# Four fused transformer layers on one core: shared experts with inner units in partitions, placed earlier, and the last gathers beside the attention

## The reference, cut to what matters

```python
sh = silu(x @ sh_gate) * (x @ sh_up) @ sh_down * sigmoid(x @ sh_gate_w)        # layer 2
z  = silu(xf @ Ws1 + bs1) * (xf @ Ws11 + bs11) @ Ws2 + bs2                      # layer 3
h  = silu(xf @ W1[e] + b1[e]) * (xf @ W11[e] + b11[e])                          # expert e
y  = y + (h @ W2[e] + b2[e]) * gates[:, e, None]
```

## Time and profile before

| what | us |
|---|---|
| median of 3 runs | 1956.16 (1954.9 to 1962.01) |
| the profiled execution | 1963.65 |
| its span, first to last instruction | 1961.8 |
| PE busy | 1400.3 (71%) |
| DVE busy | 1314.5 (67%) |
| ACT busy | 957.5 (49%) |
| POOL busy | 297.2 (15%) |

### The profile page before, as it was taken

How to read it: one execution, slowest core, us unless ns; L and a number is a source line. 1 busy time by engine, 2 the same in 40 slices (tenths; PEclk the granted TensorE clock), 3 DMA queues, 4 the chain that set the end, 5 groups by cost and what they waited for, 6 DMA issues and landing times.

```text
span 1961.8 us, 22511 instructions
## 1 busy us (share of the span) xinstructions
PE 1400.3 (71%) x6402; PEld 623.9 (32%) x6402; DVE 1314.5 (67%) x4037; ACT 957.5 (49%) x2225; POOL 297.2 (15%) x388
## 2 busy tenths in 40 slices
PE   6788888873344410453488899878898699999984
PEld 2345444441111100210134555322232234434431
DVE  5989979887888876393265566677676454555552
ACT  3888878863444433121155455444443344444452
POOL 0201010010000000047410010245205201000014
PEclk7989989897555555555598899888786799899995
DMA  3010101004100000214122223223112601111111
GB/s 111 26 49 15 51 7 63 1 1 149 60 1 1 0 1 1 63 43 135 47 50 72 67 88 95 64 59 72 41 33 80 161 20 28 25 54 45 45 30 54
DMA packets 151441, 98.44 MB, mean 50 GB/s; under 512 B 73328, under 2 KB 136117, under 8 KB 151265
## 3 DMA queue, kind: packets, MB, share of 16 engines
q1 hardware_dynamic: 143543, 84.01, 14.7%
q0 software_dynamic: 6144, 12.60, 2.3%
q10 hardware_dynamic: 1632, 0.39, 0.1%
HBM read 60.83 MB, written 35.73 MB: 49 GB/s over the span
## 4 chain that ended last, share of the span: by engine, by line
PE 46%; DVE 33%; issue 9%; ACT 6%; another core or an unknown queue 4%; DMA 1%; SPq 1%; POOL 1%; DVEq 0%; ACTq 0%; POOLq 0%
PE PS L483 38%; DVE RA L1593 5%; DVE nmx L1346 4%; PE PS L479 4%; DVE RA L1595 4%; DVE RA L1150 3%; DVE RA L1153 3%; PE PS L831 2%; DVE RB L1153 1%; DVE RB L1150 1%; DVE RA L1309 1%; DVE RA L1311 1%; PE PS L820 1%; ACT RA L1737 1%
## 5 line engine op out<-in xcount | busy, mean ns | idle before, releaser
L483 PE MATMUL PS<-RA 72*128 72x512 bf16 (+2 forms) x1360 | 463.8, 429 | 148.6 <-DVE nmx L1346 92.7
L1346 DVE TENSOR_REDUCE nmx<-PS 128x1 f32<-128x512 f32 x512 | 348.2, 685 | 257.2 <-PE PS L483 167.0
L1791 ACT ACTIVATE RA<-PS 128x512 f32<-128x512 f32 x512 | 301.7, 598 | 337.5 <-PE PS L483 276.3
L483 PEld LDWEIGHTS PS<-RA 72*128 72x128 bf16 (+3 forms) x1360 | 120.3, 103 | 456.0 <-issue 204.3
L483 PE MATMUL PS<-RA,Vs 128*32 128x512 f32 x1240 | 225.1, 721 | 0.7 <-issue 0.7
L1919 ACT ACTIVATE RA<-RA 128x8 f32<-128x8 f32 x511 | 107.5, 210 | 168.1 <-DVE RA L1593 167.2
L479 PE MATMUL PS<-ident,RB 128*128 128x128 f32 (+1 forms) x329 | 63.1, 338 | 137.6 <-DVE RB L1525 123.3
L1971 POOL DMA_INDIRECT RA<-yd,RA x96 | 93.4, 973 | 431.8 <-DMA yd<-RA 271.1
L483 PE MATMUL PS<-RB,RA 128*128 (+2 forms) x672 | 152.5, 344 | 4.6 <-DVE RA L1326 4.6
L483 PE MATMUL PS<-RB 128*128 (+3 forms) x280 | 108.7, 524 | 43.0 <-ACT RB L1893 28.8
L1150 DVE TENSOR_SCALAR RA<-PS 128x1024 f32<-128x1024 f32 x96 | 117.0, 1219 | 24.3 <-PE PS L483 24.2
(11 more groups left out here) (299 smaller groups left out, 2037.5 us busy)
## 6 DMA issues: line engine op xcount, KB each, us to landing
RA<-scr SPq DMA_DIRECT2D x288, 96.0 KB
xd<-Otok SPq DMA_DIRECT2D x36, 256.0 KB, 3.2
RA<-xd SPq DMA_DIRECT2D x72, 128.0 KB, 2.3
scr<-parts SPq DMA_DIRECT2D x48, 128.0 KB
yd<-RB SPq DMA_DIRECT2D x48, 128.0 KB, 1.8
RB<-in_L_ffn_W SPq DMA_DIRECT2D x24, 256.0 KB
scr<-parts SPq DMA_DIRECT2D x64, 48.0 KB
yd<-RA SPq DMA_DIRECT2D x48, 64.0 KB, 1.5
```

Source lines behind the costliest of these rows:

```text
L483: return e.matmul(o, l, r, start=first, stop=last)
L1346: e.tensor_reduce(nmx[:, (g + lx) % 3, c:c + 1], bank[(6, 0)[i % 2]], AX.X, ALU.max, negate=True).then_inc(*ROWMAX.up(layer, n, i))
L1791: e.activation(chunk(layer, k, i), bank[(1, 5)[i % 2]], ACT.Exp).then_inc(*EXP.up(layer, k, i))
```

## The change

It does four things.

- **Form.** A shared item's `hidden` is now four matmuls, each with 128 columns of the weights as stationary operand and the 128 tokens moving, so that the inner units come out in partitions. In layer 3 each has a bias matmul of its own behind it. The result needs no transpose: `hturned` and its copy are gone for shared items, and `down` reads what DVE gated. Such an item has three steps now.
- **Place.** `spread` takes a part of the work, a first quarter, a rate, and the earliest quarter of a task. Layer 2's items end at quarter 174, and its gathers run at 0.95 a quarter from 180 to 252. Layer 3's first `hidden` stands at quarter 226, its next items at every third quarter from 256 to 322, and the last eight from 335 to 360. The routed items of layer 3 run at 1.75 steps a quarter from 361 to 473, its gathers from 479 to 518.
- **Norms.** `READY3` is computed as 208, 220, 236, 295: blocks 1 and 2 come 11 and 19 quarters earlier. All four blocks' features use bank 2.
- **Loads.** The three loads for the shared expert of layer 3 move to quarter 200 (`shared3`). The other 24 pieces are issued two a quarter, from 348 on.

```diff
     HT = RA[:, 9984:10496].rearrange("p (u c k) -> p u c k", u=2, c=2)
+    HTs = RA[:, 9984:10496].rearrange("p (u k) -> p u k", u=2)
...
-    READY3 = (208, 231, 255, 295)
-    FEATURES3 = (2, 2, 3, 4)
-    SPLIT3 = READY3[0] + 16
+    FEATURES3 = (2, 2, 2, 2)
...
-    def expert_steps(lx):
+    def expert_steps(lx, part):
 
         nsh, G, ni = len(shared[lx]), groups[lx], items[lx]
-        steps = [[("hidden", 0)], [("gated", 0)]]
-        for i in range(ni):
+        first, end = ((0, ni), ((0, nsh), (nsh, ni))[part])[lx]
+        steps = [[("rows", r)] for r in (0, 2) if first]
+        steps += [[("turned", first + u)] for u in range(2) if first]
+        steps += [[("hidden", first)], [("gated", first)]]
+        for i in range(first, end):
             r = G * (i - nsh + 4)
-            steps.append(([("rows", r)] if r >= 0 and r % 2 == 0 and r < ntiles[lx] else []) + [("hturned", i)])
-            steps.append([("hidden", i + 1)] if i + 1 < ni else [])
-            steps.append(([("gated", i + 1)] if i + 1 < ni else []) + ([("turned", i + 2)] if nsh <= i + 2 < ni else []))
+            fetch = [("rows", r)] if end > nsh and r >= 0 and r % 2 == 0 and r < ntiles[lx] else []
+            if i >= nsh:
+                steps.append([("hturned", i)])
+            steps.append(fetch + ([("hidden", i + 1)] if i + 1 < end else []))
+            steps.append(([("gated", i + 1)] if i + 1 < end else []) + ([("turned", i + 2)] if nsh <= i + 2 < end else []))
             steps.append([("down", i)])
...
-    plan = {2: spread(expert_steps(0), 14, 2.05), 3: spread(expert_steps(1), 27, 2.25)}
-    assert not plan[2][1]
-
+    def spread(layer, steps, at, rate, earliest=lambda task: 0):
+
+        credit = 0.0
+        for tasks in steps:
+            while credit < 1.0 or at <= max([earliest(t) for t in tasks], default=0):
+                credit = min(credit + rate, 1.0 + rate)
+                at += 1
+            credit -= 1.0
+            plan[layer].setdefault(divmod(at - 1, 4), []).extend(tasks)
+        return at
+
+    plan = {2: {}, 3: {}}
+    last = spread(2, expert_steps(0, 0), 56, 2.05)
+    assert spread(2, gather_steps(0), last + 4, 0.95) <= 4 * STEPS
+    added = [max(4 * n + i for (n, i), tasks in plan[2].items() for t in tasks if t[0] == "combine" and t[1] // 16 == b) for b in range(4)]
+    READY3 = [max(added[b], 4 * (16 * b + 25) + 2, 4 * (48 + LAG) - 9) + 1 for b in range(4)]
...
+        b = task[1] // 8
+        return READY3[b] + (10 if b < 3 else 40) - 4 * LEAD
+
+    spread(3, expert_steps(1, 0), READY3[0] + 18 - 4 * LEAD, 1.0, earliest)
+    last = spread(3, expert_steps(1, 1), READY3[3] + 65 - 4 * LEAD, 1.75)
+    assert spread(3, gather_steps(1), last + 4, 0.95) <= 4 * STEPS
...
                     n, wgu, f, down, be = shared[lx][i]
-                    ins = mm(bank[bk][:, 0:2 * f], XT[:, 128 * n:128 * n + 128], wgu, True, lx == 0)
                     if lx:
-                        ins = mm(bank[bk][:, 0:2 * f], SELB[:, 128 * be:128 * be + 128], BI[:, :], False, True)
+                        wait_xt(3, n // 4)
+                    for c in range(4):
+                        o = bank[bk][:, 128 * c:128 * c + 128]
+                        ins = mm(o, wgu[:, 128 * c:128 * c + 128], XT[:, 128 * n:128 * n + 128], True, lx == 0)
+                        if lx:
+                            ins = mm(o, BI[:, 128 * c:128 * c + 128], SELB[:, 128 * be:128 * be + 128], False, True)
...
-                pe.wait_ge(HT_A, lx, i)
+                pe.wait_ge(GATED if i < nsh else HT_A, lx, i)
...
-            weights(lx, 4 * n + i - ROUTE_LATE[layer] - LOAD_FROM)
-            for task in plan[layer][0].get((n, i), ()):
-                expert_step(lx, task)
+                if layer == 2 and n == 50:
+                    shared3()
+            at_ = 4 * n + i - ROUTE_LATE[layer] - LOAD_FROM
+            for piece in range(at_, at_ + 1) if lx == 0 else range(2 * at_, 2 * at_ + 2):
+                weights(lx, piece)
...
-            if i < 2:
-                e.dma_start(w3gu[:, 16:18, 256 * i:256 * i + 256], T["L3_ffn_" + ("Ws1", "Ws11")[i]].rearrange("h (s i) -> h s i", s=2)).then_inc(*W3S.up())
...
+        def shared3():
+
+            sp.wait_ge(DOWN, 0, items[0] - 1)
+            for i in range(2):
+                e.dma_start(w3gu[:, 16:18, 256 * i:256 * i + 256], T["L3_ffn_" + ("Ws1", "Ws11")[i]].rearrange("h (s i) -> h s i", s=2)).then_inc(*W3S.up())
+            e.dma_start(w3d[:, 32:36, :], T["L3_ffn_Ws2"].rearrange("(c p) h -> p c h", p=128)).then_inc(*W3S.up("all"))
```

More of the change, by code:

```diff
@@ L339, in beside @@
                 for i in range(4):
-                    slot(16 * (b - 1) + lag + (0, 0, 1, 1)[i], (3, 3, 0, 0)[i], "values", b, i)
+                    late = b < 3 and i > 1
+                    slot(16 * (b - 1) + lag + late, 0 if late else 3, "values", b, i)
         return todo
@@ L397, in build @@
-    plan = {2: spread(expert_steps(0), 14, 2.05), 3: spread(expert_steps(1), 27, 2.25)}
-    assert not plan[2][1]
+        return [([("combine", i - 6)] if i >= 6 else []) + ([("gather", i)] if i < pairs else []) for i in range(pairs + 6)]
+    def spread(layer, steps, at, rate, earliest=lambda task: 0):
[7 more added lines that the diff above has]
+        return at
@@ L414, in both @@
                     early_step(*task)
-        for task in plan[3][1]:
-            rest(1, task)
     between = {}
@@ L980, in pe_program @@
             prep2(0, i)
-        both(step, beside_step, early3, expert_step)
+        both(step, expert_step, beside_step, early3)
     def dve_program(dve):
```

85 lines of the change are left out of this document (37 added, 48 removed).

## The result

The changed kernel takes 2001.09 us (median of 4 runs, 1997.32 to 2005.06) against 1955.53 us for the kernel before on the same chip: ratio 1.0234, 95% interval 1.0191 to 1.0276. It is slower, where the prediction said 1914 us and gave slower 4 in 100. The profiled execution took 2005.06 us, its span 2003.2.

A forecast was written before the change was run, and what follows sets the result against it. PE was taken as the bound where expert items lay (94% and 95% busy, near full clock), not between them or in the tail. -2 + 41 + 11 + 2 - 72 - 24 = -44, with 2 for bank waits -42: 1914 us, range 1887 to 1944.

The forecast's parts named there:

- the shared items beside layer 3's first quarters: Quarters 256 to 325, 24 shared items added: 142 us at 95% busy against 100.7, +41, between +12 and +64.
- rival D: Clock stays low in quarters 256 to 325 as small matmuls wait for weights: 1950 to 2005 us, chance 0.04.
- Shared items of layer 2: Layer 2's 16 shared items in the new form, without bias: -2 us, between -4 and +4.
- The denser gathers of layer 2: Layer 2's norms and gathers, same operations in the same quarters: 0, within 5 us for the denser gathers.
- Quarters 325 to 361: The other eight shared items of layer 3, in a stretch of 82.8 us: +11 us, between 0 and 21.
- Waits at quarter 361: PE waiting for the first routed rows behind the weight pieces: 2 us, between 0 and 14.
- rival C: Late rows at quarter 361 and one pause of ACT beside gathers and attention: 1936 us, chance 0.11.
- Quarters 361 to 511: Routed items of layer 3 and 38 quarters with gathers, no shared items: 284 us against 356, -72.
- The tail: Behind the last row maximum, without combines: 36 us in place of 60.3, -24, between -15 and -28.
- A: Items hide in idle time of quarters 256 to 361, +12 and 0: 1874 us, halfway 1885, chance 0.15.
- B: Nothing hides in quarters 256 to 361, +64 and +21: 1947 us, chance 0.12.
- E: The tail stays, since the last combines could still be what ends: 1938 us, chance 0.03.

The follow-up runs named there:

- e1: Kernel before with only the new form of both layers' shared items, old place and pace: 2018.58 us, ratio 1.0307.
- e5: e1 without the hidden bias of layer 3's shared items, so the computation lacks it: 1944.84 us, ratio 0.9934.
- e9: e1 with one bias product of 512 columns in place of the four of 128: 1856.26 us, ratio 1.0028.
- e13: The kernel of e7 again, as partner on one chip with e14 and e15: 1899.78 us, ratio 1.0179.
- e14: Changed kernel with four steps per layer 2 shared item and one 512-column bias product per layer 3 shared item: 1853.65 us, ratio 0.9959.
- e7: Changed kernel with an empty fourth step kept in layer 2's shared items: 1976.68 us, ratio 1.0087.
- e15: Changed kernel with the single 512-column bias product as its only edit, three steps in layer 2 kept: 1870.46 us, ratio 1.0054.
- e4: Changed kernel with both layers' shared items in the old form and layer 3's items late, 2.25 steps a quarter: 1956.05 us, ratio 0.9987.
- e11: e1 with the order of product and bias reversed in chunks 1 and 3: 1894.15 us, ratio 1.0215.
- e12: Kernel before with only layer 3's shared hidden bias cut into four 128-column products behind the one long product: 1862.16 us, ratio 1.0013.
- e6: Kernel before with layer 3's shared hidden product cut into four 128-column pieces, each with its bias, turning back kept: 2008.47 us, ratio 1.0301.
- e8: e4 with layer 3's items at 3.0 steps a quarter instead of 2.25: 1974.71 us, ratio 1.0119.
- e17: Changed kernel with four layer 2 steps, one 512-column bias product, routed items eight quarters later, first two row fetches issued at quarter 356: 1842.73 us, ratio 0.9910.

## Why the prediction was wrong

**The step that failed** stands in the part on the shared items beside layer 3's first quarters: "I take +41, since both stretches with items ran that way, and their clock was full." In those stretches hidden and its bias were products of 512 columns, and I carried their clock to a stretch where both are cut into 128. The work was sized about rightly. Length times clock, a rough measure of work at full clock, went from 100.7 x 0.80 + 82.8 x 0.61 = 131 to 177.1 x 0.79 + 105.6 x 0.64 = 207: +76, where 32 x 2.68 = 86 had been worked out. At the 0.95 or so of the forecast, 207 would have been 218 us; it was 283. That is rival D's mechanism, put at 0.04 and at 1950 us for the mild end and 2005 for the hard one. Its sum for quarters 256 to 325 holds: 142 / 0.79 = 180, and 177.1 was measured. That the whole, 2001 us, lies near its hard end is luck: the clock was that of the mild end, and layer 2 gave what was missing. D's reason, that each product waits for its weights, was not tested. e1, e5, e9, e13 and e14 show what takes the clock: the four bias products between four short f32 products. Whether by their shortness, by the changes of kind, or by both, is open.

The reason that I gave against D, the clock of 0.97 to 1.00 in the earlier trace rows, was the wrong row to ask. No stretch before holds four such pairs an item, so it bounded nothing; the bound should have been the half clock, and D a price over the whole stretch. The dear bound of an item, 0.5 us a piece for half clock, was above what the timeline shows for a pair, 0.95 - 0.58 = 0.37; but it was used for the item alone, and at half clock everything else on PE gets longer too: a bf16 product of 512 columns takes 0.39 us in the earlier trace rows and 0.61 in the tail of the changed kernel.

From the forecast's -42 to the +41 of the two profiled executions 83 us are missing: 45 in quarters 256 to 361, 39 in layer 2's quarters 56 to 256, 8 in the tail, and -9 in the rest.

**Shared items of layer 2**, -2: the form gives -2.5 (e1), so that was right. I had costed the form and not the step that it took out of the plan. Three steps for an item put the next product in front of DVE's sum (12.0 us of waits instead of 3.6), and pull items and gathers forward. With e7's edit the changed kernel gets 24 us shorter in the median (2001.1 to 1976.7, two sets), e14 against e15 says 17 in one set. That is the second largest term, and the sum had 2 us for extra waits on banks 3 and 4 in layer 3 alone.

**The denser gathers of layer 2**, 0 within 5: quarters 180 to 256 took 120.7 us in e7 and 119.7 in e4 against 112.3 before, about 8 us. In the later sets the same plan took 105.2 to 119.0 us there, against 105.2 to 106.3 in e9, e11 and e12 with the old gathers, so the size is not sure. The 132.5 of the changed kernel holds 12 us more, with the three steps.

**Quarters 325 to 361**, +11, at most 21: +22.8. The clock was 0.61 before and is 0.64, so nothing was lost here; the items were priced at full clock in a stretch that has half of it most of the time. In e14 they take 72.7 us at 0.77 against 95.4 in e13. A growth of more than 20 us stood among the signs of being wrong, and so did a clock under 0.8 in quarters 256 to 325, for D.

**Waits at quarter 361**, 2: in the changed kernel PE does not wait for the rows. That is no merit of the plan but of PE coming late: as soon as the clock is repaired the wait of rival C is there, 17 us (e14), in SyncE's queue.

**Quarters 361 to 511**, -72: -76.5 measured. The 112 quarters with the items took 227.8 us (232 and 3.3 for the values were worked out), the 38 with gathers 51.6 (48.6).

**The tail**, -24: -15.7. From the last exponential to the end 17.6 us passed (1985.59 to 2003.20), against 18.2 worked out with its 3.2. The exponentials before it took 27.0 from the last row maximum, not 18: PE did not come "out of a full clock" for long, its clock in the tail is 0.50. The chain of waits in order of time shows the rhythm, 4.2 us for four exponentials, of which PE has 3.52:

```profile
1981.39 0.60 ACT RA L1818
1982.00 0.05 issue
1982.04 3.52 PE PS L505 x11
1985.59 0.60 ACT RA L1818
```

Rivals A, B and E did not happen; B's price for quarters 256 to 361, 64 + 21, was under the 99 measured. Of C the pause did not come: from 1905 us on ACT waited three times for something outside the engines, 8.0 us in all and 4.1 at most.

## What to carry to other kernels

When a product is cut into shorter ones, ask what else in that stretch is short. Four short f32 products kept the clock at 0.96 without a bias and at 0.95 with one long bias product; with four short bias products between them it was 0.76. A bias shared by all chunks of an item fits into one product of 512 columns, and that alone was worth 60 us in quarters 364 to 421 (200.3 in e1, 140.1 in e9, two sets), and 62.5 us in quarters 256 to 361 in one set. Take a stage's clock only from rows that have the same shapes of matmuls, and price a rival of the clock over its whole stretch. Removing an operation from a step plan also removes its time slot: look who had used it to wait, and what moves forward with it.

## What the hardware showed that was not expected

The granted clock stayed at 1.2 GHz for 51 us in a row with PE busy 98%. The Trainium skill, page "TensorE: Matmul & The Clock Gate", section "What's actually happening", ties the clock to how busy PE has been. The trace doesn't bear out that the busy share alone decides: at 98% busy the clock was 1.00 in 1396.5 to 1430.8 and 0.50 in 1510.0 to 1561.5. e5, e9 and e12, set against e1, e6 and e11, show that it matters which products PE is busy with. What the chip counts, these runs don't show; and that 512 columns of bf16 a bank restore what 4 x 128 don't is measured, its cause is not.

One program has two levels 5% apart, and not by the chip: the chip of e5 to e8 gave 1955.49 us for the kernel before, and 1857.25 in the later set with e17. In quarters 0 to 56, where GpSimd scatters rows and the edits change next to nothing, e1 took 154.2 us and e9 94.0. GpSimd issues its 64 scatters of layer 2 at the same pace in both, from 872.1 to 955.0 us in e1 and from 872.5 to 955.4 in e9; but 15 quarters start beside them in e1, and 45 in e9. DVE's waits there in e1, for something that the trace places outside the engines, came to most of the 60.2 us between them:

```profile
DVE nmx L1351 <- remote: 51.6, 5, 25.9
```

e9 has no such wait among its seven longest. The pause of ACT in the earlier trace rows bears the same mark. What holds the engines in the first two sets and not in the later three stays open.
